# Row tiles 0 to 4 of a cross-attention and FFN kernel in a written-out order, with the first value product in four idle banks

## The reference, cut to what matters

```
x = x + xattn(layernorm(x), ctx)        # 8 heads of 64; q = xn Wq, k = ctx Wk, v = ctx Wv
                                        # softmax(q k / 8) v, then @ Wo + bo
x = x + ffn(layernorm(x))               # xq = fake_quant(x, whole-tensor maximum)
                                        # h = fake_quant(silu(xq Wg) * (xq Wu), whole-tensor maximum)
                                        # h @ Wd; Wg, Wu, Wd rounded by row
```

## Time and profile before

| what | us |
|---|---|
| time, median of 3 runs | 547.78 |
| lowest and highest | 546.44, 548.42 |
| the profiled execution, device time | 547.3 |
| its span | 545.5 |
| PE busy in the span | 528.1 |
| DVE, ACT, POOL busy | 475.3, 294.2, 231.8 |
| granted TensorE clock, share of full | 0.999 |

### The profile page before, as it was taken

How to read it: one execution, slowest core, us unless ns; L and a number is a source line. 1 busy time by engine, 2 the same in 40 slices (tenths; PEclk the granted TensorE clock), 3 DMA queues, 4 the chain that set the end, 5 groups by cost and what they waited for, 6 DMA issues and landing times.

```text
span 545.5 us, 8102 instructions
## 1 busy us (share of the span) xinstructions
PE 528.1 (97%) x2740; PEld 355.9 (65%) x2740; DVE 475.3 (87%) x879; ACT 294.2 (54%) x414; POOL 231.8 (42%) x349
## 2 busy tenths in 40 slices
PE   8989889999999999999999899999999999999997
PEld 7868678787888878888788644444444445544444
DVE  4966988999989899898989799999999988899884
ACT  4834645556465654554534646555545533999500
POOL 4385858769596895856553000000000000055442
PEclk9999999999999999999999999999999999999999
DMA  8809375765668465545949955850442220399987
GB/s 315 275 41 301 92 210 171 226 215 160 214 212 272 143 216 178 178 129 165 203 88 313 282 122 242 283 141 22 116 117 44 72 38 5 123 328 234 159 106 127
DMA packets 82943, 93.83 MB, mean 172 GB/s; under 512 B 47085, under 2 KB 50157, under 8 KB 82645
## 3 DMA queue, kind: packets, MB, share of 16 engines
q1 hardware_dynamic: 77877, 84.13, 49.9%
q0 software_dynamic: 4320, 7.87, 9.6%
q10 hardware_dynamic: 704, 1.31, 0.7%
HBM read 47.51 MB, written 37.78 MB: 156 GB/s over the span
## 4 chain that ended last, share of the span: by engine, by line
PE 73%; DVE 12%; SPq 6%; DMA 3%; issue 2%; ACT 1%; POOL 1%; ACTq 0%; DVEq 0%; POOLq 0%
PE SP L1137 13%; PE QO L1137 13%; PE QO L192 5%; PE QO L194 4%; PE QO L193 4%; SPq L37 4%; PE SP L463 4%; PE QO L1294 4%; PE PTP L1294 3%; PE SP L1294 3%; SPq L41 2%; PE MI L583 2%; PE MI L582 2%; PE MI L581 2%; PE WOP L1294 2%
## 5 line engine op out<-in xcount | busy, mean ns | idle before, releaser
L45 POOL DMA_DIRECT2D out<-n2b x30 | 30.3, 1045 | 207.4 <-DVE n2b L1327 207.4
L1144 ACT ACTIVATE sil<-QO,fsc 128x512 f32<-128x512 f32 x87 | 59.8, 687 | 70.9 <-PE QO L1137 69.3
L1137 PE MATMUL SP<-nT,wgu 128*128 128x512 bf16 x340 | 87.3, 379 | 0.4
L1137 PE MATMUL QO<-nT,wgu 128*128 128x512 bf16 x340 | 87.3, 379 | 0.1
L1148 DVE SCALAR_TENSOR_TENSOR h<-SP,fsc,sil 128x512 f32<-128x512 f32 x87 | 65.1, 748 | 8.7 <-PE SP L1137 7.1
L504 POOL TENSOR_TENSOR PN<-P,rs 128x512 f32<-128x512 f32 x64 | 44.3, 714 | 50.2 <-DVE rs L496 50.2
L1151 DVE TENSOR_REDUCE hmx<-h 128x1 f32<-128x512 f32 x87 | 59.7, 686 | 3.0
L487 ACT ACTIVATE P<-P,r 128x616 f32<-128x616 f32 x32 | 26.0, 812 | 63.7 <-DVE P L483 63.7
L1137 PEld LDWEIGHTS SP<-nT,wgu 128*128 128x128 bf16 x340 | 32.9, 98 | 41.4 <-DVE h L1148 2.5
L1137 PEld LDWEIGHTS QO<-nT,wgu 128*128 128x128 bf16 x340 | 33.2, 98 | 40.2 <-ACT sil L1144 0.3
L192 PE MATMUL QO<-xTs,wqs 128*128 128x512 f32 x124 | 50.4, 407 | 2.3 <-DVE xTs L223 2.0
(11 more groups left out here) (224 smaller groups left out, 1203.3 us busy)
## 6 DMA issues: line engine op xcount, KB each, us to landing
xTr<-in_xT SPq DMA_DIRECT2D x8, 1024.0 KB, 7.9
xn<-in_x SPq DMA_DIRECT2D x32, 256.0 KB, 3.8
out<-x SPq DMA_DIRECT2D x32, 256.0 KB, 2.9
n_rows<-n SPq DMA_DIRECT2D x32, 256.0 KB, 2.7
n2b<-n_rows SPq DMA_DIRECT2D x32, 256.0 KB, 3.8
out<-n2b POOLq DMA_DIRECT2D x30, 256.0 KB, 6.5
h_spill<-h SPq DMA_DIRECT2D x2, 2816.0 KB, 9.3
h<-h_spill SPq DMA_DIRECT2D x6, 768.0 KB, 7.2
```

What stands on the lines that cost most here:

```text
L1137: m = e.matmul(ps, wv_[:, k, col:col + 128], nT[:, b % 2, :, k, :], start=(k == 0), stop=(k == 3))
L1144: t_sil[n] = add("act", lambda e: e.activation(sil[:, n % SR, :], gp, ACT.Silu, scale=fsc[:, ic:ic + 1]), [t_g[n], t_fs, t_h.get(n - SR)], ...
```

## The change

Steps 0 to 3 of `attend` are gone, with the exceptions for them, and their pieces and most of those of step 4 up to the scores of tile 4 stand written out ahead of `attend(4)`. The core of the diff, cut:

```diff
-        def v_rows(r):
+        def v_mm(r):
...
+            v_at[r] = qo_bank(pairs, 512, m, [t_wvl, t_ctxl])
+        def v_out(r):
...
+            th = add("act", lambda e: e.activation(hi, bank, ACT.Copy), [t, t_v.get(r - 2)], "qo_hi")
+            tl = add("dve", lambda e: e.tensor_tensor(lo, bank, hi.bitcast(f32), ALU.subtract),
+                     [th, t_v.get(r - 2)], "qo_lo")
...
+            if n in (0, 4):
+                add("pe", lambda e: fn(e, 0, 3), [t_qm[b, 2], *t_kl, *free])
+                t_S[n] = add("pe", lambda e: fn(e, 3, 4), [t_q[b]], "S_mm")
...
-            free = t_sub[30] if n == 30 else t_pl[29] if n == 31 else t_pl.get(n - 1)
+            free = t_sub[30] if n == 30 else t_pl[29] if n == 31 else t_oss[0, 1] if n == 4 else t_pl.get(n - 1)
...
-            banks = []
-            for j in range(2):
+            banks = [] if b else [(None, MI[:, :], ()), (None, WOP[:, :], (t_c,)),
+                                  (None, PTP[:, 0:512], ()), (None, PTP[:, 512:1024], ())]
+            for j in range(2 if b else 0):
...
-        for at, tile in ((4, 22), (8, 23), (12, 24), (16, 25)):
+        for at, tile in ((8, 22), (12, 23), (16, 24), (20, 25)):
...
+        S(0)
+        v_mm(0)
+        soft(0, "max", "sub", "exp")
+        split_lo(1, 0, "dve")
+        v_out(0)
+        v_mm(1)
+        S(1)
+        soft(0, "sum", "rec", "norm")
+        soft(1, "max", "sub")
+        v_out(1)
+        load_vb(0)
+        v_mm(2)
+        soft(1, "exp")
+        S(2)
+        split_lo(1, 2, "dve")
+        t_xT[2] = load_xT(2, t_xTs[1])
...
+        v_out(2)
+        v_mm(3)
+        soft(2, "exp")
+        PT(0)
+        PT_high(0)
+        v_out(3)
+        q_chunk(1, 0)
...
+        q_chunk(1, 1)
...
+        v_mm(4)
+        v_out(4)
+        PT(2)
+        PT_high(2)
+        q_chunk(1, 2)
...
+        w_tops(0)
+        w_round(0)
+        w_integer(0)
+        w_load(2)
+        PT(3)
+        PT_high(3)
+        q_chunk(1, 3)
...
+        PV_rest(0)
+        S(4)
+        split_lo(2, 2, "dve")
+        soft(4, "max", "sub")
+        split_lo(2, 3, "dve")
+        PV(0, 2)
+        soft(4, "exp")
+        PV(0, 3)
+        soft(4, "sum", "rec", "norm")
+        PV(0, 0)
+        PV(0, 1)
+        w_tops(1)
+        w_round(1)
+        w_integer(1)
+        w_load(3)
+        q_chunk(2, 0)
+        q_chunk(2, 1)
+        row_stats(5)
+        first_bias(4)
+        w_tops(2)
+        w_round(2)
+        w_integer(2)
+        row_stats(6)
...
-        for s in range(28):
+        for s in range(4, 28):
             attend(s)
```

More of the change, by code:

```diff
@@ L456, in S, with fn @@
                 free = [t_sub[29] if n == 31 else t_sub.get(n - 1)]
-            if t == 1 and b > 0:
+            if t == 1 and b > 1:
                 free += [t_oss[b - 1, 2], t_oss[b - 1, 3]]
-            def fn(e):
-                for j in range(4):
+            def fn(e, j0=0, j1=4):
+                for j in range(j0, j1):
                     o = S_bank(n)[:, (j // 2) * 512 + (j % 2) * 154:(j // 2) * 512 + (j % 2) * 154 + 154]
@@ L542, in PV_rest @@
                 banks.append((at, state["banks"][at], state["free"][at]))
-            for k in range(2):
-                banks.append((None, SP[:, 512 * k:512 * k + 512], (t_sub[min(4 * b + 4, NT - 1)],)))
+            if b:
+                for k in range(2):
+                    banks.append((None, SP[:, 512 * k:512 * k + 512], (t_sub[min(4 * b + 4, NT - 1)],)))
             pv_at[b] = banks
@@ L717, in block_kernel, with soft, row_stats, w_tops @@
         t_pz = add("pool", lambda e: e.memset(PN[:, :, 512:640], 0.0), [t_ctxl, t_wkl], "c_pz")
+        def soft(n, *steps):
+            for step in steps:
+                {"max": soft_max, "sub": soft_sub, "exp": soft_exp, "sum": soft_sum, "rec": soft_rec,
+                 "norm": soft_norm}[step](n)
+        def row_stats(n):
+            first_stats(n)
+            first_aggr(n)
+            first_scale(n)
+        def w_tops(i):
+            w_top(i)
+            w_scale(i)
+            w_inverse(i)
@@ new lines, in block_kernel @@
+        v_mm(3)
[4 more added lines that the diff above has]
+        q_chunk(1, 0)
+        soft(2, "sum", "rec", "norm")
+        first_bias(1)
+        PT_low(0)
+        S(3)
+        row_stats(3)
+        soft(3, "max", "sub")
+        PT(1)
+        PT_high(1)
+        soft(3, "exp")
+        q_chunk(1, 1)
+        PT_low(1)
+        soft(3, "sum", "rec", "norm")
+        first_bias(2)
+        first_bias(3)
+        v_mm(4)
+        v_out(4)
+        t_flat = [t_v[4], t_v[3], t_wol, ("qo_mm", c.count["qo_mm"])]
@@ L887, in attend @@
                 when("n2", normed, s - 6)
-            if s == 0:
-                v_rows(3)
-            if s == 1:
-                for n in range(3):
-                    first_bias(n)
             when("s", soft_norm, s + 1)
@@ L895, in attend @@
             if more:
-                for k in range(2 if s == 2 else 3):
+                for k in range(3):
                     split_lo(b + 2, k)
```

130 lines of the change are left out of this document (49 added, 81 removed).

## The result

| what | before, us | after, us |
|---|---|---|
| time, median of 3 runs | 547.78 | 554.04 |
| lowest and highest | 546.44, 548.42 | 553.81, 554.98 |
| profiled execution | 547.3 | 553.81 |
| its span | 545.5 | 552.0 |
| PE busy | 528.1 | 530.7 |

The changed kernel is slower: ratio 1.0123, with an interval from 1.0104 to 1.0141. The forecast was 549.4 with a range up to 552.0, so the change costs more than the forecast's range allowed, on the side of its two slower rivals (551.6 and 552.4) and beyond both.

What follows compares the result with a forecast made beforehand. PE was taken as the bound. New waits against those gained put the first output product at 80.05 instead of 78.48, 1.6 later: 547.3 + 1.6 = 548.9, plus 0.5 for the median, 549.4 us; range 545.6 to 552.0.

Steps and rivals of the forecast that it cites:

- wait ahead of scores 1: PE's wait for tile 0's softmax, 1.81 us before, disappears because value products 0 and 1 fill it.
- ahead of query product (1,0): PE waits about 0.9 us because DVE copies the low half of value 2 late, at 43.4.
- store 2 issued, landed: Store of value product 2 stands behind vbd and xTr loads on SP: issued about 49.7, landed 55.7.
- wait ahead of transposes 3, their start: PE waits 1.75 us for tile 2's halves, held up on ACT by the store's landing; start 57.8.
- ahead of query product (2,0): Batch 2's wait for the low halves on DVE stays, at 1.35 us.
- ahead of scores 6, released at: PE waits 4.8 us for tile 5's subtraction, behind DVE's weight rows and statistics; released at 79.1.
- DVE waits for the load of row 3: Weight row 3's load needs row 1's buffer, so its data come late; the chain ends at 79.1.
- down-weight rows: Wide rows handled at steps 9, 13, 17 and 21 cost nothing; at most about 1 us in batch 5.
- a rival's 0.12: Clock falls to 1.2 GHz in the 4.8 us wait; products behind lose up to 2.2: 551.6, chance 0.12.
- late-store rival: Store of value product 2 lands after 57, at 58.7, 3.0 us later than taken: 552.4, chance 0.10.
- The offset: PE's 1.6 us lateness at the first output product is carried unchanged to the end.
- The fill: Rival: no wait for the store, DVE ahead of its list, tile 6's scores wait only 2.0: 544.8, chance 0.14.

Runs made afterwards that it cites:

- run 6: Kernel before with only the down-weight rows handled one batch later: 547.44 us, ratio 1.0001.
- run 1: Changed kernel with query product (2,1) put back between the scores of tiles 5 and 6: 555.0 us, ratio 1.0143.
- run 2: Changed kernel with weight rows 0 and 1 handled ahead of value product 4, loads of rows 2 and 3 behind it: 552.79 us, ratio 1.0107.
- run 4: Changed kernel with small matmuls filling both long PE waits, 14 ahead of tile 3's transposes and 17 ahead of tile 6's scores: 551.9 us, ratio 1.0097.
- run 9: The changed kernel itself, measured again beside the kernel before: 555.24 us, ratio 1.0145.
- run 10: Changed kernel with 14 small matmuls filling only the wait ahead of tile 3's transposes: 553.64 us, ratio 1.0109.
- run 11: Changed kernel with 17 small matmuls filling only the wait ahead of tile 6's scores: 553.52 us, ratio 1.011.
- run 5: Changed kernel with query product (2,1) back between the scores, weight rows 0 and 1 early, stores ahead of vbd and xTr loads: 546.62 us, ratio 0.998.
- run 7: Kernel before with only the first value product moved to banks MI, WOP and the halves of PTP: 550.08 us, ratio 1.0042.
- run 12: Kernel of run 5 with tile 7's statistics and weight row 3 moved behind tile 5's subtraction on DVE: 547.49 us, ratio 0.9998.
- run 8: Changed kernel with stores ahead of vbd and xTr loads and weight rows 0 and 1 early, scores still side by side: 547.12 us, ratio 0.9992.
- run 3: Changed kernel with the vbd and batch 2 xTr loads issued behind the stores of value products 2 and 3: 549.78 us, ratio 1.0036.

## Why the prediction was wrong

Step by step, as the prediction put them:

| step | predicted | trace of after |
|---|---|---|
| wait ahead of scores 1 | none | none |
| ahead of query product (1,0) | 0.9 | 0.31 |
| store 2 issued, landed | 49.7, 55.7 | 49.70, 56.43 |
| wait ahead of transposes 3, their start | 1.75, 57.8 | 3.08, 58.71 |
| ahead of query product (2,0) | 1.35 | 0.43 |
| ahead of scores 6, released at | 4.8, 79.1 | 4.78, 81.23 |
| DVE waits for the load of row 3 | yes | 0.54 |
| first output product | 80.05 | 83.27 |
| scores behind it, against before | +1.6 | +6.05 |
| down-weight rows | nothing | nothing (run 6) |

- **The waits** were right in place and in cause, and near in sum: 8.8 us (without the 0.2 ahead of scores 0, which didn't come) against 8.60. That the sums are so close is partly luck: the first long wait was 1.3 longer than forecast, outside the 1 to 2.5 that the prediction gave it, and two short ones 0.6 and 0.9 shorter. The walk along the lists found both new waits, including the one through the buffer of weight row 1.
- **The failed step is the clock.** The forecast took the products behind the waits of 1.75 and 4.8 at the prices of the earlier trace rows, all measured at full rate, and so put the loss of rate at nothing. The trace has 4.0 us of it (3.8 against the same pieces behind a wait at full rate). The argument was that "a wait of 4.8 has no example there". That is no evidence for full rate, and the only row with slow matmuls, was at the program's start, with no matmuls ahead of it. That row was weak evidence too, because the clock in the trace reads 1.00 there. Still, nothing in the rows spoke for full rate, and the loss should have had more than a rival's 0.12. The rule cited there, the Trainium skill (TensorE: Matmul & The Clock Gate, "Why this matters for your kernels"), says that idle stretches between bursts put the clock back to half, and the trace of after agrees: 0.50 from 59 to 62 and from 80 to 85.
- **Its price was counted once.** The rival had up to 2.2 us for one wait, 551.6 in all. There were two long waits, and the trace has 1.65 and 2.35. With both, the forecast is 549.4 + 4.0 = 553.4, against 554.04. At the scores behind the output product it adds up: +1.6 forecast, 4.0 for the clock, 0.9 for the later start of transposes 3, 0.4 less elsewhere, and +6.05 measured.
- **Store 2** was the smaller error. ACT was released by it at 56.5, not 55.7. In the six other traces with this order (runs 1, 2, 4 and 9 to 11) it was at 57.5 to 58.2: SP took 10.25 to 10.57 for the 12 loads of vbd, not 9.54, so that the store was issued at 50.5 to 51.0, and its landing took 6.7 to 7.7. The late-store rival was to be decided by a landing after 57. The trace of the result has 56.43, the other six are all later than 57. So this term was too small by 0.7 in the one trace and by 1.7 to 2.5 in the others. Which of the two the untraced executions of the result had isn't known.
- **The offset**, +6.05 behind the first output product, is +6.17 at the first full FFN product: carried nearly unchanged when PE is late, as assumed. Run 5 shows that it isn't symmetric. PE 2.3 early keeps 0.76. The waits of PE and DVE in the next batch fit the reading that DVE and the transfers aren't early with it, but no run tests that.
- **The fill** was given little chance for the right reason, DVE's weight rows. Run 2 takes one of the three away, and with it DVE's wait for the load of row 3, and the wait halves. Run 1 restores the cover and nothing comes of it.
- **The two sums** of the prediction, 3.0 more of waits but only 1.6 in the starts, were put down to 0.16 in each of five waits. That is 0.8 and leaves 0.6 of the difference open. The forecast goes by the starts, so nothing hangs on it.

## What to carry to other kernels

When a change trades several short waits of TensorE for one long one, don't compare their sums. Price the matmuls behind a long wait at half rate until the rows show that the clock is back, once for every such wait. Here that was 1.5 to 2.7 us for each wait of 2.45 or more, and the slow stretch lasted longer in some executions than in others. Read the mean granted clock of every execution too: it shows a loss of rate that the one trace may not have. Before a list is rewritten, look at what each store stands behind on the issuing queue, and who needs its buffer: here moving 12 small loads and a large one behind the stores was worth over 4 us. And don't count a lead in full: here 2.3 us of it had become 0.76 by the next phase.

## What the runs showed of the hardware that was not expected

- The length of a wait alone doesn't tell whether the clock falls. It stayed at 1.00 in the traces of before (waits up to 1.81), run 5 (1.46), run 7 (2.25) and run 12 (2.21), fell behind 1.81 in run 6, and fell behind 2.45 and 2.46 in runs 8 and 2. Behind these last two, of equal length, the slow matmuls began at different points: in run 8 already in the scores (1.58), in run 2 only in the product behind them (1.32, then 0.63).
- The kernel before isn't free of it either. Of its 66 executions beside the other kernels, 19 had a mean granted clock of 0.997 or less. On the second chip, 10 such executions have a median of 548.6, the 25 others 547.0. Where the clock fell in them wasn't traced; run 6 shows one place.
- The 12 small transfers of vbd keep SP busy for 9.3 to 10.6 us, some 0.8 each (9.49 before; 9.54 in the changed kernel and 10.25 to 10.57 in the six other traces with its order; 9.75 to 10.09 behind the stores in runs 3, 5, 8 and 12; 9.33 for batch 1 in run 5). What is called behind them is issued that much later, and not equally late in each run.
- In the two measurements of the changed kernel this difference grew along the chain. The store was issued 1.1 us later (50.84 against 49.70), the transposes of tile 3 started 1.25 later, the output product 2.6 later (85.85 against 83.27), and the medians are 1.2 apart. The second half of that is the clock again: in run 9 it stayed at half longer behind the first wait, so that scores 4 came 6.94 behind transposes 3 and not 5.91, and the second wait was 0.33 longer.
